# A quantised gated feed-forward stage: the down matrix turned behind the up products, magnitudes in fewer passes, two blocks and the first down tile in halves

## What is computed

```python
def act_qdq(x):                       # one scale for the whole tensor
    scale = jnp.maximum(jnp.max(jnp.abs(x)) / 32767.0, 1e-12)
    return jnp.clip(jnp.round(x / scale), -32768.0, 32767.0) * scale

x = act_qdq(x)
up = act_qdq(x @ lpbq_dequant(w_up).T)
gate = act_qdq(x @ lpbq_dequant(w_gate).T)
sig = fixed_qdq_u16(jax.nn.sigmoid(gate))
gate = act_qdq(gate * sig)
o = act_qdq(gate * up)
return o @ lpbq_dequant(w_down).T
```

## Time and profile before

| | |
|---|---|
| median of 3 runs | 758.8 us (758.45 to 759.79) |
| profiled execution, its time | 758.51 us |
| profiled execution, its span | 756.8 us |
| mean granted TensorE clock | 0.988 |
| busy over the span | PE 93%, ACT 72%, DVE 65%, PEld 52%, POOL 21% |
| HBM traffic | 27.94 MB read, 4.46 MB written |

### The profile page before, as it was taken

One profiled execution on the slowest core, in us unless ns is written; L12 is line 12 of the kernel. 1 busy time (PEld: TensorE's weight loads), 2 busy tenths in 40 slices (PEclk: granted clock), 3 DMA queues, 4 the chain that ended last, 5 costly groups with the idle time before them and its releaser, 6 DMA issues.

```text
span 756.8 us, 10995 instructions
## 1 busy us (share of the span) xinstructions
PE 702.8 (93%) x3914; PEld 391.1 (52%) x3914; DVE 491.1 (65%) x1162; ACT 548.2 (72%) x998; POOL 159.8 (21%) x224
## 2 busy tenths in 40 slices
PE   7989999999999999999999999979998899992897
PEld 5642222212222225889888887644555644441686
DVE  3885755763413325588447665759977877988786
ACT  2659999999999995564142435799887533899991
POOL 2642143201010000104263232333220100000022
PEclk9999999999999999999999999999999999997899
DMA  8113212131256151303336000001100000000002
GB/s 257 43 29 41 44 30 70 29 98 29 37 135 206 29 148 48 112 2 112 110 112 223 1 1 0 2 19 66 43 1 1 2 0 1 0 0 1 0 29 83
DMA packets 56973, 41.48 MB, mean 55 GB/s; under 512 B 37106, under 2 KB 53720, under 8 KB 56792
## 3 DMA queue, kind: packets, MB, share of 16 engines
q1 hardware_dynamic: 56744, 40.65, 19.3%
q10 hardware_dynamic: 176, 0.14, 0.1%
HBM read 27.94 MB, written 4.46 MB: 43 GB/s over the span
## 4 chain that ended last, share of the span: by engine, by line
PE 47%; ACT 29%; DVE 13%; issue 8%; POOL 3%; POOLq 0%; DVEq 0%; ACTq 0%
ACT arena L678 18%; PE banks L2251 8%; PE banks L2013 7%; PE banks L2029 6%; PE banks L1695 4%; PE banks L1681 3%; ACT arena L803 2%; PE banks L1874 2%; DVE arena L1520 2%; PE banks L1665 2%; PE banks L2141 2%; DVE arena L1060 1%; PE banks L2043 1%; DVE arena L1068 1%; PE banks L1909 1%
## 5 line engine op out<-in xcount | busy, mean ns | idle before, releaser
L678 ACT ACTIVATE arena<-banks 128x1024 f32<-128x1024 f32 x256 | 235.4, 1182 | 0.6 <-PE banks L1681 0.5
L1695 PE MATMUL banks<-arena 128*32 128x512 f32 x1024 | 136.4, 604 | 0.5
L1681 PE MATMUL banks<-arena 64*128 64x512 f16 x512 | 83.6, 383 | 4.7 <-ACT arena L678 1.6
L2251 PE MATMUL banks<-arena 128*128 128x512 f32 x192 | 83.0, 593 | 0.2 <-ACT arena L861 0.2
L1681 PEld LDWEIGHTS banks<-arena 64*128 64x128 f16 x512 | 20.1, 93 | 104.6 <-ACT arena L678 95.8
L803 ACT ACTIVATE arena<-banks,arena 128x77 f32<-128x77 f32 x256 | 64.5, 373 | 12.5 <-DVE arena L1410 12.5
L431 POOL TENSOR_SCALAR arena<-arena 128x2 f32<-128x2 f32 (+2 forms) x39 | 11.7, 299 | 259.4 <-DVE arena L1063 259.4
L759 ACT ACTIVATE arena<-banks,arena 128x256 f32<-128x256 f32 x64 | 26.9, 471 | 49.3 <-PE banks L2013 49.3
L2251 PEld LDWEIGHTS banks<-arena 128*128 128x128 f32 x192 | 36.2, 190 | 46.3 <-issue 42.8
L2029 PE MATMUL banks<-arena 128*128 128x256 f32 x256 | 56.5, 380 | 1.2 <-ACT arena L700 1.2
L2013 PE MATMUL banks<-arena 128*128 128x256 f32 x256 | 56.2, 379 | 0.0
(11 more groups left out here) (267 smaller groups left out, 1227.2 us busy)
## 6 DMA issues: line engine op xcount, KB each, us to landing
arena<-in_L_ffn_w SPq DMA_DIRECT2D x16, 1024.0 KB, 7.5
w_kept<-arena SPq DMA_DIRECT2D x3, 768.0 KB, 3.6
arena<-w_kept SPq DMA_DIRECT2D x3, 768.0 KB, 4.6
arena<-in_x SPq DMA_DIRECT2D x4, 512.0 KB, 6.3
out_x<-arena SPq DMA_DIRECT2D x3, 512.0 KB, 2.9
arena<-in_L_ffn_b SPq DMA_DIRECT2D x1, 1024.0 KB, 13.0
arena<-in_L_ffn_w_gate SPq DMA_DIRECT2D x1, 768.0 KB, 7.3
arena<-in_L_ffn_w_up SPq DMA_DIRECT2D x1, 768.0 KB, 9.1
```

Source lines behind the costliest of these rows:

```text
L678: act.activation(PT[(TB * u + kt) % 3][:, half], PS[:, 2 * (n % 3):2 * (n % 3) + 2, :], ACT.Exp, scale=DH ** -0.5 / QK_UP ** 2).then_inc(s ...
L1681: mm = pe.matmul(bank(2 * (n % 3) + h), KT[u % 2][64 * h:64 * h + 64, P * kt:P * kt + P], QT[u % 2][64 * h:64 * h + 64, 512 * half:512 * h ...
L1695: mm = pe.matmul(PS[32 * j:32 * j + 32, 6, :], VS[w][:, kt, h, :], PT[(TB * u + kt) % 3][:, half, h, :], start=(kt == 0), stop=(kt == TB - 1))
L2251: mm = pe.matmul(bank(2 + n % 4), (wgT if n < IC * G4 else wuT)[:, k, P * c:P * c + P], XT[:, k, 512 * g:512 * g + 512], start=(k == 0), s ...
```

## The change

WQ_LAST ends with turn 5; turns 6 to 8 stand behind the last up product on PE, and their copies behind the last UI part on ACT. The raw down matrix gets a buffer of its own, `wd_raw`, over the buffers `rdS` and `qTx` of cross attention; SP loads it when the last use of these is over (`xa_ptr` 32), in place of its load beside that of up. The wait of PE for all nine copies stands behind the warming matmuls, which read up weights and are eleven. The up magnitudes are six passes, two of which take six blocks of two groups and of one group. The last gated block is made to `gi` in halves, the second one behind UI part c == 3; the last UI part is two halves. ACT makes two pairs ahead, and pair t + 2 behind copy t. Tile 0 is rounded in two halves of three blocks; DVE copies the first half to f32, ACT the second, and PE starts on the first. Two pairs of semaphores around the maximum of x are merged (each wait is on the same event as before); this part of the diff is left out.

```diff
-WQ_LAST = ((0, 1), (2, 3), (4,), (5, 6, 7, 8))
+WQ_LAST = ((0, 1), (2, 3), (4,), (5,))
-WARMING = 10
+UP_SETS = ((0, 2, IC), (2 * IC, 1, IC), (3 * IC, 1, 2), (3 * IC + 2, 1, 2), (3 * IC + 4, 1, 1), (3 * IC + 5, 1, 1))
+WARMING = 11
+FIRST = IC // 2
+HALF_ROW = T * P // 2
-    + tuple((c, slice(0, T * P)) for c in range(2, IC))
+    + tuple((c, slice(0, T * P)) for c in range(2, IC - 1)) + ((IC - 1, slice(0, HALF_ROW)), (IC - 1, slice(HALF_ROW, T * P)))
...
+        l0x_f = Bump(10544, 13120)
+        wd_raw = l0x_f(IC, D)
...
-            sp.dma_start(wraw1[:, 12:18], w_kept[:, 12:18]).then_inc(sem("w_down_in"), 16)
             sp.wait_ge(sem("ln_d2"), G4)
             sp.dma_start(wraw1[:, 0:6], w_kept[:, 0:6]).then_inc(sem("w_gate_in"), 16)
+            sp.wait_ge(sem("xa_ptr"), UX)
+            sp.dma_start(wd_raw, w_kept[:, 12:18]).then_inc(sem("w_down_in"), 16)
...
             g2_magnitude(IC - 2)
-            g2_magnitude(IC - 1)
+            g2_magnitude(IC - 1, slice(0, T * P // 2))
             act.wait_ge(sem("f_u_scale"), 1)
             for c, part in UI_PARTS:
                 act.activation(ui[:, c, part], UF[:, c, part], ACT.Abs, scale=sc[:, 26:27]).then_inc(sem("f_ui"), 1)
+                if c == 3:
+                    g2_magnitude(IC - 1, slice(HALF_ROW, T * P))
+            for n in range(6, 9):
+                wq_evac(n)
...
                     act.wait_ge(sem("f_oi"), t - 3 - t // 4 + 1)
+                    if t == 4:
+                        act.wait_ge(sem("f_first"), 2)
...
-            for t in range(3):
+            for t in range(2):
                 f_signed(t)
...
                     act.wait_ge(sem("f_o"), t + 1)
-                    act.activation(UF[:, :, P * t:P * t + P], g_signed[t % 4], ACT.Copy).then_inc(sem("f_oi"), 1)
-                if t + 3 < T:
-                    f_signed(t + 3)
+                    part = slice(0 if t else FIRST, IC)
+                    act.activation(UF[:, part, P * t:P * t + P], g_signed[t % 4][:, part], ACT.Copy).then_inc(sem("f_oi"), 1)
+                if t + 2 < T:
+                    f_signed(t + 2)
...
-            for n in range(IC * G4, 2 * IC * G4 - 2, 2):
-                dve.wait_ge(sem("gu"), n + 2)
-                g, c = n // IC % G4, n % IC
-                magnitude(mxs[:, n:n + 2], UF[:, c:c + 2, 512 * g:512 * g + 512])
-            for n in range(2 * IC * G4 - 2, 2 * IC * G4):
-                ins = evacuated(n)
+            for i, (n, groups, blocks) in enumerate(UP_SETS):
+                dve.wait_ge(sem("gu"), IC * G4 + n + groups * blocks)
+                g, c = n // IC, n % IC
+                ins = dve.tensor_reduce(mxs[:, i:i + 1], UF[:, c:c + blocks, 512 * g:512 * g + 512 * groups], AX.XY, ALU.max, apply_absolute_value=True)
...
                 dve.wait_ge(sem("f_signed"), t + 1)
+                if t == 0:
+                    g, u = g_signed[0], u_signed[0]
+                    dve.scalar_tensor_tensor(g[:, 0:FIRST], g[:, 0:FIRST], sc[:, 34:35], u[:, 0:FIRST], ALU.mult, ALU.mult).then_inc(sem("f_first"), 1)
+                    dve.wait_ge(sem("f_first"), 1)
+                    dve.tensor_copy(UF[:, 0:FIRST, 0:P], g[:, 0:FIRST]).then_inc(sem("f_first"), 1)
+                    dve.scalar_tensor_tensor(g[:, FIRST:IC], g[:, FIRST:IC], sc[:, 34:35], u[:, FIRST:IC], ALU.mult, ALU.mult).then_inc(sem("f_o"), 1)
+                    return
...
-            pe.wait_ge(sem("wqT"), 9)
+            for n in range(6, 9):
+                wq_turn(n)
             pe.wait_ge(sem("f_ui"), IC + 1)
             for n in range(WARMING):
-                pe.matmul(bank(7)[:, 0:D], ident, wdT[:, n % IC, :], start=True, stop=True)
+                pe.matmul(bank(7)[:, 0:D], ident, wuT[:, 1, 0:D], start=True, stop=True)
+            pe.wait_ge(sem("wqT"), 9)
             for t in range(T):
...
-                else:
+                elif t:
                     pe.wait_ge(sem("f_oi"), t + 1 - (t + 1) // 4)
                 for c in range(IC):
+                    if t == 0 and c == 0:
+                        pe.wait_ge(sem("f_first"), 2)
+                    if t == 0 and c == FIRST:
+                        pe.wait_ge(sem("f_oi"), 1)
```

More of the change, by code:

```diff
@@ L851, in _, with g2_magnitude @@
                     wq_evac(n)
-            def g2_magnitude(c):
+            def g2_magnitude(c, part=slice(0, T * P)):
                 act.wait_ge(sem("f_k3"), 1)
-                act.activation(gi[:, c, :], GF[:, c, :], ACT.Abs, scale=sc[:, 31:32])
+                act.activation(gi[:, c, part], GF[:, c, part], ACT.Abs, scale=sc[:, 31:32])
             for n in range(2 * IC * G4):
@@ L1520, in magnitude @@
                 return dve.tensor_reduce(dst, src, AX.X, ALU.max, apply_absolute_value=True)
-            dve.tensor_reduce(sc[:, 0:1], xmax, AX.X, ALU.max).then_inc(sem("x_amax"), 1)
+            dve.tensor_reduce(sc[:, 0:1], xmax, AX.X, ALU.max).then_inc(sem("x_top"), 1)
             dve.memset(ones_row[0:1, :], 1.0)
-            dve.wait_ge(sem("x_amax_row"), 1)
+            dve.wait_ge(sem("x_spread"), 1)
             dve.tensor_reduce(sc[0:1, 38:39], bank(2)[0:1, 0:P], AX.X, ALU.max).then_inc(sem("x_top"), 1)
-            dve.wait_ge(sem("x_top_all"), 1)
+            dve.wait_ge(sem("x_spread"), 2)
             link(dve.tensor_copy(sc[:, 10:11], bank(3)[:, 0:1]))
@@ L1584, in _ @@
             dve.tensor_scalar(sc[:, 37:38], sc[:, 31:32], -1.0, None, ALU.mult).then_inc(sem("f_k3"), 1)
-            for n in range(IC * G4, 2 * IC * G4 - 2, 2):
-                dve.wait_ge(sem("gu"), n + 2)
-                g, c = n // IC % G4, n % IC
-                magnitude(mxs[:, n:n + 2], UF[:, c:c + 2, 512 * g:512 * g + 512])
-            for n in range(2 * IC * G4 - 2, 2 * IC * G4):
-                ins = evacuated(n)
+            for i, (n, groups, blocks) in enumerate(UP_SETS):
+                dve.wait_ge(sem("gu"), IC * G4 + n + groups * blocks)
+                g, c = n // IC, n % IC
+                ins = dve.tensor_reduce(mxs[:, i:i + 1], UF[:, c:c + blocks, 512 * g:512 * g + 512 * groups], AX.XY, ALU.max, apply_absolute_value=True)
             link(ins)
-            dve.tensor_reduce(sc[:, 2:3], mxs[:, IC * G4:2 * IC * G4], AX.X, ALU.max).then_inc(sem("amax"), 1)
+            dve.tensor_reduce(sc[:, 2:3], mxs[:, 0:len(UP_SETS)], AX.X, ALU.max).then_inc(sem("amax"), 1)
             dve.wait_ge(sem("gmax"), 3)
@@ L2159, in wq_turn @@
                         c, k = i // KD, i % KD
-                        src = wraw1[:, 12:18].rearrange("p (k c) d -> p k (c d)", k=KD)[:, k, P * c:P * c + P]
+                        src = wd_raw.rearrange("p (k c) d -> p k (c d)", k=KD)[:, k, P * c:P * c + P]
                     mm = pe.transpose(bank(n % 2)[:, P * j:P * j + P], src, ident)
@@ L2222, in x_top @@
             def x_top():
-                pe.wait_ge(sem("x_amax"), 1)
-                pe.transpose(bank(2)[0:1, 0:P], sc[:, 0:1], ident).then_inc(sem("x_amax_row"), 1)
                 pe.wait_ge(sem("x_top"), 1)
-                pe.matmul(bank(3)[:, 0:1], ones_row[0:1, :], sc[0:1, 38:39], start=True, stop=True).then_inc(sem("x_top_all"), 1)
+                pe.transpose(bank(2)[0:1, 0:P], sc[:, 0:1], ident).then_inc(sem("x_spread"), 1)
+                pe.wait_ge(sem("x_top"), 2)
+                pe.matmul(bank(3)[:, 0:1], ones_row[0:1, :], sc[0:1, 38:39], start=True, stop=True).then_inc(sem("x_spread"), 1)
             for g in range(G4):
```

## The result

| | before | after |
|---|---|---|
| median, runs on the same chip | 759.29 us (758.45 to 760.05, 6 runs) | 764.35 us (763.84 to 765.43, 6 runs) |
| ratio after to before | | 1.0066, 95% interval 1.0056 to 1.0076 |
| profiled execution, span | 756.8 us | 761.8 us |
| mean granted TensorE clock | 0.988 | 0.978 |

The kernel is 5.1 us slower (764.35 for 759.29); the forecast was 763.2 us, 4.4 above the 758.8 that it started from. The two profiled executions don't reach the last stage at the same moment, so a time inside that stage is best counted from the first gate product: 602.25 before, 600.38 after. From there to the end of the last normalisation pass 152.4 us before (602.25 to 754.62) and 159.3 after (to 759.64): 6.9 longer. The earlier start of the gate products gives 1.55 back.

The account below looks back on a forecast made before the run. ACT's copies and pairs, then DVE's list behind pair 15, were taken to set the end. Front terms and round 0 (-1.43) plus the look-ahead (+6.0) gave +4.6 us; 763.2 us was written, range 759.5 to 765.6.

Parts of the forecast that it names:

- Start of the gate products: First gate product on PE follows the first rounding, no longer turns 7 and 8: 1.63 us sooner, no second wait.
- Up magnitudes: DVE's passes over the up products: seven instructions fewer at 0.061 us each, -0.43 us, with 1.0 as the bound.
- UI parts: ACT's UI parts before round 0: a short wait for block 4 and block 5 in halves cost +0.26 us.
- Turns 6 to 8: Turns behind the up products: turn 8 starts at 702.1, copy 8 ends at 703.8, pair 0 hidden with 0.6 us to spare.
- Warming: PE's eleven matmuls and two records behind turn 8: 7.8 us from 703.3, so tile 0 starts at 711.1.
- rival C: PE's longer idling lowers its clock to 1.2 GHz in warming, perhaps in tiles: 764.1, up to 766 us; chance 0.10.
- Tile 0 in halves: Round 0 in two halves of 0.51 us, half f32 copy about 0.3; +0.37 us in the sum.
- The look-ahead: ACT two pairs ahead, not three: +2.04 of work, stalls at copies 8 (+1.6) and 12 (+2.36), together +6.0 us.
- Tail: DVE's list behind pair 15, 16.1 us long, waits for nobody but POOL and shifts whole.
- Rival A: Not slower: DVE's rounds reach ACT in time at copies 8 and 12, so no stalls; +0.1, 758.6 us; chance 0.10.
- B: Rival: the front gains nothing, as PE's start follows DVE or ACT another way; +1.6, 764.7 us; chance 0.05.
- D: Rival: faster, as PE sets the end and tile 0 starts at 707.0; 755.7 us; chance 0.05.

Follow-up runs that it names:

- a_warm4: The changed kernel with 4 warming matmuls instead of 11; 764.97 us, ratio 1.0073 to the kernel before.
- b_ahead2: The kernel before with nothing but ScalarE's look-ahead cut to two pairs; 764.90 us, ratio 1.0070 to the kernel before.
- a_ahead3: The changed kernel with the look-ahead of three pairs put back; 758.93 us, ratio 0.9992 to the kernel before.
- a_order: The changed kernel with round 8 moved ahead of VectorE's first sum and round 12 ahead of the second; 761.84 us, ratio 1.0022 to the kernel before.
- b_turns: The kernel before with the turns part alone: own buffer and late load for the down matrix, turns 6 to 8 and their copies later; 757.34 us, ratio 0.9974.
- c_early: The changed kernel with look-ahead three, tile 0 and UI block 5 whole, copies 6 and 7 made early; 758.59 us, ratio 0.9981 to the kernel before.
- b_load: The kernel before with only the down matrix loaded late into its own buffer; 759.42 us, ratio 0.9999.
- b_passes: The kernel before with only the up magnitudes in six passes; 758.32 us, ratio 0.9999.
- b_warm18: The kernel before with 18 warming matmuls instead of 10 and nothing else; 758.49 us, ratio 0.9994.
- c_warm19: The version with the early copies (c_early) with 19 warming matmuls instead of 11; 756.43 us, ratio 0.9965 to the kernel before.

## Why the prediction was right

**Start of the gate products.** -1.63 forecast, -1.55 found; no second wait.

**Up magnitudes.** -0.43 forecast, 13.59 - 13.17 = 0.42 found, in the change and alone. The row's reading of 0.061 us an instruction held. The figure of the Trainium skill (VectorE: DVE Perf Modes, The TRN2 errata), about 150 cycles, would have given 1.1 us: it stands for the duration of one instruction (one pass of 1024 lasted 1.209 us against 1.067 for its elements), not for the distance between starts of instructions that follow each other.

**UI parts.** +0.26 forecast. From the start of the UI parts to round 0 pass 17.78 us (688.27 to 706.05) for 17.42 before (690.48 to 707.90): +0.36.

**Turns 6 to 8.** As forecast: turn 8 started at 702.15 (702.1), pair 0 was in time. **Warming** was sized 0.7 us too long (7.11 for 7.8), and tile 0 started at 709.98, not 711.1; nothing hung on it, which a_warm4 shows from the other side. The granted clock was 0.50 from 703 to 706, 0.63 from 706 to 708 and 1.00 from 708 to 710: warming began at the lower level, as rival C has it, but the clock was back before tile 0.

**Tile 0 in halves.** The sum had +0.37; found +0.72 (1.75 less 1.03). This is the term that was mis-sized. The half f32 copy on VectorE took 0.55 us, as much as the 0.56 of a whole tile and not 0.3, and the two halves of the round 0.62 and 0.61 for 0.51.

**The look-ahead.** +6.0 forecast. From copy 0 to the end of pair 15 pass 35.7 us (707.82 to 743.50) for 29.5 before (708.95 to 738.49): +6.1. The stalls came out at 1.59 and 2.89 for 1.56 (5.60 - 4.04) and 2.86. They were pure arithmetic on two distances of the old trace, and b_ahead2, a_ahead3 and a_order show the mechanism from three sides.

**Tail.** 16.13 us behind pair 15 before, 16.14 after, as forecast.

**Sum.** The forecast was +4.6 on the profiled execution. The terms as found give -1.55 - 0.42 + 0.36 + 0.72 + 6.1 = +5.2, and 0.1 more lies between the first gate product and the up passes: 5.3. The spans differ by 5.0, because the execution after reached the stage 0.3 us sooner; the medians differ by 5.1. All the errors of the terms have the same sign, so none hid another, and the largest is the halves' 0.35. The forecast of 763.2 was 1.15 us short in absolute time; 0.5 of that is only that the kernel before has a median of 759.29 here and not 758.8. Rival A fell with the two stalls, B with the 1.55, C and D with a_warm4.

**What stays open.** The ratios of several experiments lie below what the front and the length of the stage in their traces say: those of a_ahead3, a_order, b_ahead2, b_turns and c_early by 0.15 to 0.2% (b_turns 0.9974 for 0.9990, a_ahead3 0.9992 for 1.0007), those of b_load and b_passes by 0.2 and 0.3%. Only b_turns and b_ahead2 have the trace's figure within their interval. Two things on record bear on it.

First, the stages are compared with a profiled execution of the kernel before that took 758.51 us, while its medians beside these runs are 0.7 to 1.1 us higher. Its 29 times beside a_order lie in groups: ten up to 758.94 with a granted clock of 0.986 to 0.988, thirteen from 759.09 to 759.98, eleven of them at 0.982 to 0.985, and six from 762.6 up at 0.977 to 0.982. That the kernel loses clock ahead of tile 0 in part of its executions fits, but the groups don't show it: the profiled execution of b_load did lose clock there, and has 758.82 us and a mean of 0.988.

Second, the way to the stage varies as well. From 570 to 580 us, behind a wait of TensorE for ScalarE of 2.17 us, the granted clock is 0.83 in eleven of the fourteen kept traces and 1.00 in three, b_load, b_turns and a_order; eight 128x256 records took 3.27 us in the kernel before and 1.89 in these. The first gate product then comes 1.3 us sooner, beyond the 1.55 of the turns. In b_turns that makes up the difference: its profiled execution is 2.06 us below that of the kernel before, 1.55 - 0.8 + 1.3. In b_load the same 1.3 us hides most of the 1.6 us of its longer stage, so its level time doesn't show that the late load changes nothing. All three traces with the full clock have the late load; seven others have it too and don't have the full clock, and none of the four without the load does. Whether the load or chance decides is not shown. b_warm18, the only run that tried the clock ahead of tile 0 in the kernel before, has too wide an interval.

## What to carry to other kernels

Where two engines hand tiles to each other in written-out order, look for the longest piece of work that stands between two hand-overs on the one, and count what the other has in hand at that point: its look-ahead has to cover that piece, not the mean load. A pair taken off the front of a busy list is not saved, it is paid behind, and here with a stall on top. And a part of a stage that starts earlier is worth what arrives at the engine that sets the end: by the traces, of the 1.55 us of the turns 0.8 arrived in b_turns and nothing in c_early, where the copies were made in idle time but TensorE lost its clock; with longer warming (c_warm19) all of it arrived.

## What the runs showed of the hardware that was not expected

Small differences ahead of tile 0 went with TensorE's clock. With idle times of 3.46 (b_ahead2) and 3.66 us (before) between warming and tile 0 the down records took 41.7 to 41.8 us; with 4.06, 4.24 and 5.03 us (c_early, b_load, b_passes) they took 43.4 to 44.4, at 0.52 to 0.60 granted over the first 4 us. The same 20 warming records lasted 5.96 to 7.53 us in different executions, which moves that idle time by itself; the executions with the longer idle time are those with the shorter warming, and no run parts the two. The idle time alone does not decide: near 573 us a wait of 2.17 us was followed by a granted clock of 0.83 in eleven traces and of 1.00 in three. The Trainium skill (TensorE: Matmul & The Clock Gate, Why this matters for your kernels) has the rule that short idle gaps keep the clock; the rows ahead of tile 0 agree with it in kind, the eleven traces near 573 us do not.

An f32 copy of a 128x384 int16 tile on VectorE took 0.55 us, that of 128x768 0.56. Why the half is not shorter was not tried.
